# Second attention: which of its small steps run on GpSimd and which on VectorE

## The reference

```
Q, K, V   = xn @ wq, xn @ wk, xn @ wv              16 heads of 8
local     = windowed causal softmax attention, window 32
GQ        = xn @ wgq;  latents = mean of each 4 tokens of xn -> 64 latents
GK, GV    = latents @ wgk, latents @ wgv           8 heads of 8
remote    = causal softmax attention of GQ over the latents, @ r_out_w
x        += (sigmoid(gate_l) * local + sigmoid(gate_r) * remote) @ w_out + MoE(xn)
MoE(xn)   = shared expert * sigmoid(xn @ shared_gate_w)
            + top-8 of 64 experts, weights w / sum(w), at most 64 tokens an expert
```

## Time and profile before

| | us |
|---|---|
| median of 3 runs | 1795.48 (1791.98 to 1797.09) |
| the profiled execution's own time | 1784.54 |
| its span, first to last instruction | 1782.8 |
| second attention, first xT to last pooled batch | 985.8 to 1576.6 |

### The profile page before, as it was taken

One profiled execution on the slowest core, in us unless ns is written; L12 is line 12 of the kernel. 1 busy time (PEld: TensorE's weight loads), 2 busy tenths in 40 slices (PEclk: granted clock), 3 DMA queues, 4 the chain that ended last, 5 costly groups with the idle time before them and its releaser, 6 DMA issues. The chain is left out here.

```text
span 1782.8 us, 43704 instructions
## 1 busy us (share of the span) xinstructions
PE 1623.9 (91%) x13929; PEld 1198.6 (67%) x13931; DVE 1143.2 (64%) x2695; ACT 1007.7 (57%) x2546; POOL 832.5 (47%) x1413
## 2 busy tenths in 40 slices
PE   4799999999999999989996899999999999995883
PEld 4655555555555555547996688888888888884772
DVE  3356555555555555543443699999999999995661
ACT  3355555555555555543442677777777777762341
POOL 5235555555555555553444444444444444412664
PEclk9999999999999999999998799999999999996676
DMA  7412221222222212212221112112111111115444
GB/s 194 128 31 76 55 55 54 54 54 54 54 54 54 54 54 54 54 47 83 65 65 44 31 43 43 40 38 43 41 40 41 43 40 41 43 35 109 96 84 118
DMA packets 207886, 107.45 MB, mean 60 GB/s; under 512 B 102745, under 2 KB 196250, under 8 KB 207770
## 3 DMA queue, kind: packets, MB, share of 16 engines
q1 hardware_dynamic: 197594, 93.16, 20.9%
q0 software_dynamic: 10240, 13.64, 3.5%
HBM read 61.85 MB, written 40.16 MB: 57 GB/s over the span
## 5 line engine op out<-in xcount | busy, mean ns | idle before, releaser
L662 POOL TENSOR_SCALAR_AFFINE_SELECT probs<-probs 128x512 f32<-128x512 f32 x256 | 183.8, 742 | 157.4 <-ACT probs L1446 157.3
L899 DVE TENSOR_REDUCE mneg<-bankS 128x2 f32<-128x256 f32 x256 | 107.5, 420 | 215.1 <-PE bankS L1778 193.7
L1446 ACT ACTIVATE probs<-bankT 128x1024 f32<-128x1024 f32 x128 | 131.1, 1025 | 180.7 <-PE bankT L1798 180.7
L900 DVE TENSOR_REDUCE mneg<-bankS 128x2 f32<-128x512 f32 x256 | 174.6, 682 | 0.0
L1437 ACT ACTIVATE qT<-bankA,bd 128x256 f32<-128x256 f32 x256 | 107.7, 474 | 89.8 <-PE bankA L1760 89.8
L1760 PE MATMUL bankA<-xnT,wd 128*128 128x256 f32 x512 | 149.6, 416 | 0.0
L655 POOL CAST qb<-qT 128x256 bf16<-128x256 f32 x256 | 97.7, 400 | 95.2 <-ACT qT L1437 95.0
L1812 PE MATMUL bankB<-probs,vaug 128*64 128x512 f32 x512 | 140.2, 626 | 1.1 <-ACT yT L1453 1.0
L1795 PE MATMUL bankT<-qT,kT 37*128 37x512 f32 x512 | 136.7, 610 | 3.5 <-DMA qT<-mT 1.8
L1542 ACT ACTIVATE pe<-pr 128x768 f32<-128x768 f32 x128 | 108.2, 845 | 28.2 <-DVE pr L1240 26.0
L1246 DVE STREAM_TRANSPOSE pt<-pe 128x768 f32<-128x768 f32 x128 | 123.8, 967 | 0.4 <-ACT pe L1542 0.2
(11 more groups left out here) (317 smaller groups left out, 4640.8 us busy)
## 6 DMA issues: line engine op xcount, KB each, us to landing
rzb<-reciprocals SPq DMA_DIRECT2D x128, 128.0 KB
yT<-yT SPq DMA_DIRECT2D x64, 128.0 KB
xtab<-tab SPq DMA_DIRECT2D x32, 192.0 KB, 2.0
xs_sorted<-zeros SPq DMA_DIRECT2D x1, 4608.0 KB, 19.2
qT<-xs_sorted SPq DMA_DIRECT2D x36, 128.0 KB, 2.1
ys_sorted<-qT SPq DMA_DIRECT2D x36, 128.0 KB, 1.8
value_rows<-vrow SPq DMA_DIRECT2D x32, 128.0 KB, 1.8
vx<-value_rows SPq DMA_DIRECT2D x256, 16.0 KB, 1.8
```

The source lines that it names most:

```text
L662: pool.affine_select(out=blocks, in_=blocks, compare_op=ALU.is_ge, fill=0.0, base=0, pattern=[[0, 4], [1, P]], channel_multiplier=-1).then ...
L899: dve.tensor_reduce(mneg[:, n.half, 0, :, j], bankS[:, :, 0:128], AX.X, ALU.max, negate=True)
L900: dve.tensor_reduce(mneg[:, n.half, 1, :, j], bankS[:, :, 128:384], AX.X, ALU.max, negate=True).then_inc(S["red_done"], 1)
L1446: act.activation(pT[:, g % 2].rearrange("p e j t -> p e (j t)"), bankT[:, 0:2, :], ACT.Exp, scale=SCALE0).then_inc(S["exp_done"], 1)
```

## The change

Five small steps of the second attention go from DVE to POOL. The pooling of latents is made of two additions of neighbours, with the new tile `xq` between. The two reciprocals are made with a power of -1, from a new constant tile `minus`. The sum of the gated parts moves as it is. Of the weighing, the reduction over the experts stays on DVE (`weight_sum`), and the mask product, `sgc`, the inversion and the product with it move. POOL gets a `step1` of its own, in which the moved functions stand among the old ones: pooling (n), stream (m), gated sum (p), weighing (n), norm (m), weights (n), scaling of rows (b), stream added (b), gather (k = b + 3). The semaphore `x1_copied` goes (its signal is now in `x1_done`) and `top8` comes.

```
@@ gpsimd
             def normalise_rows(b):
+                pool.wait_ge(S["rows_sb"], 2 * b.b + 2)
+                passed(pool)
+                pool.tensor_tensor(recd[:, :, :].rearrange("p s h -> p (s h)"), dens[:, :, :].rearrange("p s h -> p (s h)"),
+                                   minus[:, 0:1].to_broadcast([P, 4 * SL]), ALU.pow).then_inc(S["rd_done"], 1)
                 pool.wait_ge(S["rows_sb"], 2 * b.b + 3)
                 pool.wait_ge(S["rd_done"], b.b + 1)
...
+            def pool_latents(n):
+                pool.wait_ge(S["tT_sb"], n.b + 1)
+                passed(pool)
+                pairs = xT1[:, n.half, :].rearrange("p (m k) -> p m k", k=2)
+                pool.tensor_tensor(xq[:, :], pairs[:, :, 0], pairs[:, :, 1], ALU.add).then_inc(S["xp_done"], 1)
+                pool.wait_ge(S["xp_done"], n.b * 2 + 1)
+                pairs = xq[:, :].rearrange("p (m k) -> p m k", k=2)
+                pool.tensor_tensor(xp[:, n.half, :], pairs[:, :, 0], pairs[:, :, 1], ALU.add).then_inc(S["xp_done"], 1)
+
+            def gated_sum(b):
+                pool.wait_ge(S["comb"], b.b * 2 + 2)
+                passed(pool)
+                pool.tensor_tensor(aT[:, :], at1[:, :], at2[:, :], ALU.add).then_inc(S["aT_done"], 1)
+
+            def weigh(n):
+                u = n.half
+                pool.wait_ge(S["ex_done"], n.b + 1)
+                pool.wait_ge(S["M_done"], n.b + 1)
+                passed(pool)
+                pool.tensor_scalar(sgc[:, u, :], tsg[:, :], 0.5, 0.5, ALU.mult, ALU.add)
+                pool.tensor_tensor(exl[:, :, :], exl[:, :, :], mb[:, u], ALU.mult).then_inc(S["rstep"], 1)
+
+            def weights(n):
+                u = n.half
+                pool.wait_ge(S["rstep"], n.b * 3 + 2)
+                passed(pool)
+                pool.tensor_tensor(wsum[:, 1, :], wsum[:, 0, :], minus[:, 0:1].to_broadcast([P, 2]), ALU.pow).then_inc(S["rstep"], 1)
+                pool.wait_ge(S["rstep"], n.b * 3 + 3)
+                pool.tensor_tensor(tab[:, u, :, C:C + E1], exl[:, :, :], wsum[:, 1, :].unsqueeze(2).to_broadcast([P, 2, E1]),
+                                   ALU.mult).then_inc(S["tab_done"], 1)
+
+            def step1(b, p, n, m, k):
+                if n:
+                    pool_latents(n)
+                if m:
+                    stream1(m)
+                if p:
+                    gated_sum(p)
+                if n:
+                    weigh(n)
+                if m:
+                    norm1(m, True)
+                if n:
+                    weights(n)
+                if b:
                     normalise_rows(b)
                     add_stream(b)
-                    gather(b.next().next().next())
+                if k:
+                    gather(k)
...
             stream1(second)
+            pool_latents(first)
+            weigh(first)
+            norm1(second, False)
+            weights(first)
+            gather(Batch(1, 0))
@@ vector
-            def pool_latents(n):
-                dve.wait_ge(S["tT_sb"], n.b + 1)
-                dve.tensor_reduce(xp[:, n.half, :], xT1[:, n.half, :].rearrange("p (n k) -> p n k", k=CHUNK), AX.X,
-                                  ALU.add).then_inc(S["xp_done"], 1)
...
-            def weigh(n):
...
+            def weight_sum(n):
+                dve.wait_ge(S["rstep"], n.b * 3 + 1)
+                passed(dve)
                 dve.tensor_reduce(wsum[:, 0, :], exl[:, :, :], AX.X, ALU.add).then_inc(S["rstep"], 1)
...
-            def invert1(b):
-                dve.wait_ge(S["rows_sb"], 2 * b.b + 2)
-                dve.reciprocal(recd[:, :, :], dens[:, :, :]).then_inc(S["rd_done"], 1)
...
-                dve.wait_ge(S["comb"], b.b * 2 + 2)
-                dve.tensor_tensor(aT[:, :], at1[:, :], at2[:, :], ALU.add).then_inc(S["aT_done"], 1)
```

More of the change, by code:

```diff
@@ L543, in _ @@
             pool.memset(halfneg[:, :], -0.5)
+            pool.memset(minus[:, :], -1.0)
             pool.memset(owr[:, :], 0.0).then_inc(S["zeroed"], 1)
@@ L829, in _ @@
[L829 to L840, removed]
@@ L841, in _ @@
-            add_stream(Batch(LOOP, 1))
+                if k:
+                    gather(k)
+            first, second = Batch(0, 0), Batch(0, 1)
+            gather(first)
+            gather(second)
+            clear()
+            stream1(first)
+            norm1(first, False)
+            stream1(second)
+            pool_latents(first)
[3 more added lines that the diff above has]
+            gather(Batch(1, 0))
+            step1(first, None, second, Batch(1, 0), Batch(1, 1))
@@ new lines, in _ @@
+            step1(second, first, Batch(1, 0), Batch(1, 1), Batch(2, 0))
+            with pool.Fori(1, LOOP - 1) as i:
+                step1(Batch(i, 0), Batch(i, 0).before(), Batch(i, 1), Batch(i + 1, 0), Batch(i + 1, 1))
+                step1(Batch(i, 1), Batch(i, 0), Batch(i + 1, 0), Batch(i + 1, 1), Batch(i + 2, 0))
+            step1(Batch(LOOP - 1, 0), Batch(LOOP - 2, 1), Batch(LOOP - 1, 1), Batch(LOOP, 0), Batch(LOOP, 1))
+            step1(Batch(LOOP - 1, 1), Batch(LOOP - 1, 0), Batch(LOOP, 0), Batch(LOOP, 1), None)
@@ L843, in _ @@
+            step1(Batch(LOOP, 0), Batch(LOOP - 1, 1), Batch(LOOP, 1), None, None)
+            step1(Batch(LOOP, 1), Batch(LOOP, 0), None, None, None)
+            gated_sum(Batch(LOOP, 1))
             for u in range(2):
@@ L1216, in route @@
                 dve.tensor_tensor(mb[:, u], lg1[:, :, 0:E1], lgr[:, :, :], ALU.not_equal).then_inc(S["M_done"], 1)
-            def weigh(n):
-                u = n.half
-                dve.wait_ge(S["ex_done"], n.b + 1)
-                dve.wait_ge(S["M_done"], n.b + 1)
-                dve.tensor_tensor(exl[:, :, :], exl[:, :, :], mb[:, u], ALU.mult).then_inc(S["rstep"], 1)
-                dve.wait_ge(S["rstep"], n.b * RSTEPS + 2)
-                dve.tensor_reduce(wsum[:, 0, :], exl[:, :, :], AX.X, ALU.add).then_inc(S["rstep"], 1)
-                dve.wait_ge(S["rstep"], n.b * RSTEPS + 3)
-                dve.reciprocal(wsum[:, 1, :], wsum[:, 0, :]).then_inc(S["rstep"], 1)
-                dve.wait_ge(S["rstep"], n.b * RSTEPS + 4)
-                dve.tensor_scalar(sgc[:, u, :], tsg[:, :], 0.5, 0.5, ALU.mult, ALU.add)
-                dve.tensor_tensor(tab[:, u, :, C:C + E1], exl[:, :, :], wsum[:, 1, :].unsqueeze(2).to_broadcast([P, 2, E1]),
-                                  ALU.mult).then_inc(S["tab_done"], 1)
+            def weight_sum(n):
+                dve.wait_ge(S["rstep"], n.b * 3 + 1)
+                passed(dve)
+                dve.tensor_reduce(wsum[:, 0, :], exl[:, :, :], AX.X, ALU.add).then_inc(S["rstep"], 1)
             def shift(b, g):
@@ L1308, in step1 @@
                 if n:
-                    weigh(n)
+                    weight_sum(n)
                 if b:
```

24 lines of the change are left out of this document (11 added, 13 removed).

## The result

The changed kernel takes 2108.01 us (median of 4 runs, 2102.68 to 2111.21), the kernel before, run beside it, 1796.28: a ratio of 1.174, 95% interval 1.170 to 1.177, slower by 17%. The forecast was 2137 with a range of 2000 to 2235. The profiled execution has a span of 2100.6 in place of 1782.8 (+317.8) and a mean granted clock of 0.896 of full speed in place of 0.955.

What follows compares the result with a forecast made beforehand. Loop bound by DVE for two thirds and PE for one, 19.15 us a step. Added: 29 steps x 10.95 = 318, last two 15, tail 5.9 and 0.4, start 3, together 342; 1784.5 to 2126.5, plus 10.9: 2137 us, range 2000 to 2235.

Steps and rivals of the forecast that it cites:

- The power, 8.0 us: POOL's inversion of the denominators over 128x48: 0.41 us fixed plus 0.158 a column, 8.0 us against 0.45 on DVE.
- The walk: One loop step followed through POOL's queue from the fourth probability transpose: 30.1 us a step, 10.95 more than before.
- the 0.2 for the clock: PE idle from +6.1 to +13.4, then remote, queries and scores at up to twice their time; 0.2 us a step added.
- start and end: Start: weigh(0) before norm1(1), pooling of batch 1 behind a gather, some 3 us; tail: rows scaled 5.9 later, slower sum 0.4.
- the last two steps: Loop steps without a gather: 2 x (10.95 - 3.5) = 15 us more.
- the median: Median of the runs shown taken as 10.9 us above the profiled execution, raising 2126.5 to 2137.
- the path through pooling and ACT's copies: Pooling behind the gather until +18.1, ACT's copies to +28.0, last exponential and fourth transpose: +29.9, setting the step.
- that through the gated sum: Gathered rows +18.8, stream +21.0, gated sum +21.9, projection, DVE's last addition +23.1, next fourth transpose about +29.6.
- the two pieces that leave the chain: DVE's pooling reduction, 0.42 us, and final gated sum, 0.40: 25 us if nothing else moved; not subtracted in the forecast.
- The first rival: Power over 48 columns costs 0.5 to 2 us: step 22.6 at the lower bound, 1899 us, up to 1940; 10%.
- The signs: In the loop: POOL busy two thirds, DVE idle 8 us, ACT 10, clock below 1.00, chain of waits mostly POOL.
- a curve that flattens: Power below 8.0 us: cheap, 0.5 to 2 us, 10%; or slope falling with length, 3 to 6.5 us, 1970 to 2085, 9%.

Runs made afterwards that it cites:

- experiment 5: Changed kernel with a probe ahead of the second attention, POOL powers over 1 to 96 columns, twice each, and additions: 2193.06 us, one run.
- Experiment 4: Changed kernel with the gated sum put ahead of the next batch's stream in POOL's queue: 2086.57 us, ratio 1.165 to the kernel before.
- experiment 3: Kernel before with only the denominators' inversion as POOL's power, plus unread products on PE in its wait: 22 products 2079.03 us, 12 products 1967.39 us.
- Experiment 1: Changed kernel with the inversion of the denominators back on DVE as a reciprocal: 1896.78 us, ratio 1.058 to the kernel before.
- experiment 6: Changed kernel, inversion on DVE, pooling before gather, sum before stream: 1794.29 us; sum also on DVE: 1782.90; kernel before with only pooling on POOL, before gather: 1784.41.
- experiment 2: Kernel before with one move alone, the denominators inverted by POOL's power: 2044.35 us, ratio 1.142.
- experiments 6 to 8: After experiment 6: its 1782.90 us kernel with index copies ahead of pooling, 1778.18 us; then changed kernel with POOL and DVE operations timed side by side, 2123.97 us.

## Why the prediction was right, and where it was not

**The power, 8.0 us.** Right: 8010 ns. Two rows of one operation at two sizes gave slope and offset, and experiment 5 shows the same line from 1 to 96 columns. The Trainium skill's 2.6 cycles an element (GPSIMD Engine Reference, section 3.1) fails here by far: 0.159 us at 1.2 GHz are an estimated 190 cycles a column.

**The walk.** From the end of the fourth transpose, forecast and trace: weights done +3.7, +3.3; power +11.8, +11.3; rows scaled +12.75, +12.3; gather +17.0, +16.4; pooling +18.1, +17.2; ACT's string of copies over +28.0, +26.8. Each is a little early: POOL did not wait ahead of the weights' power and only 0.08 behind it (0.35 was allowed for both), the products over 128x128 took 0.40 and not 0.46, pooling 0.77 and not 1.1, and ACT's string 9.5 and not 9.85. The end from there was 0.4 longer than forecast, for the wait of the next paragraph, and the 0.2 for the clock is not seen. Together that is the 1.08 us by which the step was over-estimated (30.1 forecast, 29.02 measured). Over 29 steps it is some 31 us. The rest nearly cancels, which is luck: start and end cost 18.6 and not 9.3 (6.6 of it in stages that the change doesn't touch), the last two steps 13 and not 15, and the median lay 5.3 above the profiled execution where I had added 10.9. So the time was 29 too high.

**Which way round is the longer.** Named wrongly. I gave the path through pooling and ACT's copies +29.9 and that through the gated sum +29.6. In the trace ACT waits 0.41 for DVE ahead of the last exponential, and DVE's last addition, which ends at +22.3 (forecast +23.1), had waited for the projection of the gated sum:

```profile
1421.26 0.42 DVE L1310 TENSOR_TENSOR res<-bankT,res 128x256 f32<-128x256 f32 x1 [0.71 <-PE bankT L2132]
```

```profile
1426.52 0.84 ACT L1568 ACTIVATE pe<-pr 128x768 f32<-128x768 f32 x1 [0.41 <-DVE pr L1275]
```

Experiment 4 takes the sum's path away and gains just about that, 0.45. For the time it makes no difference here; for someone who wants to mend the kernel it is the difference between moving pooling and moving the sum.

**The clock.** I saw the idle stretch and the half clock after it, and then wrote that what runs slowly has slack until +20, and added 0.2. For the power alone that is too small: experiment 3 shows 2.6 us a step (27.3 against 24.7), since DVE waits for the scores in bank S, and my term would have been off by 75 us. For the whole change the slack was there: ACT's string starts when POOL has pooled and then runs without a gap, and PE is back at full clock before the gated sum comes. So the stretch lies under pooling's wait (power alone 27.3 with the clock in it, the whole change 29.0). That is read from the trace; no run keeps PE busy in the changed kernel.

**What the other moves cost.** The earlier trace rows offered 0.8 us a step for the two pieces that leave the chain. Against it stood the place in POOL's queue: pooling behind a gather that holds the queue for 3.5 us. Experiment 1 measures that as +3.3 a step, experiment 6 as the same 3.3 given back by a reordering. The first rival (a step of 22.6 for a cheap power) is borne out in kind by 22.4, but the closeness is partly luck: its walk gives 21.9 for a power that costs nothing and has no term for the clock, and in experiment 1 the clock fell in 19 of 29 steps.

**The signs.** POOL is busy 68% of a step, DVE waits 7.4 us a step and ACT 10, both for POOL, and the step's clock is 0.82, all as forecast. One sign did not come: the page's chain of waits is not mostly POOL (PE 4% of the span, POOL 3%). It goes back only to the last steps of the stage, whose powers it holds, and so tells nothing of the loop; the step from one scaling to the next had to serve in its place.

**Chances.** Between cheap and dear power I kept 19% for a curve that flattens. Two rows at 2 and 8 columns can't rule it out, so that was fair.

## What to carry to other kernels

Before an operation moves to another engine, find that very operation there at two sizes: an addition of 48 columns and a power of 48 columns differ by thirty on GpSimd. Then read the target's queue and not its busy share: an engine with 10 us to spare in 19 is late for everybody if the new work stands behind a gather or ahead of what another engine waits for, and another order of that queue was worth some 100 us here, with the same work in it. Where another engine leaves TensorE idle, count with its products after the gap at half speed: after a wait of 6 us it was so in every step (experiment 2), after one of 2 us in 19 of 29 (experiment 1).

## What the runs showed of the hardware

- An operation of VectorE over 128 columns between SBUF tiles, 0.22 to 0.29 us alone, is held up until GpSimd's operation has ended where that is an addition, a scaling by constants or a copy. It costs 0.4 to 0.5 us more beside an addition of 256 columns and 0.2 beside a scaling or copy (experiments 6 to 8). GpSimd's power, 2.3 us for 12 columns, does not do this, nor its scaling of the normed batch, beside which VectorE's product stayed at 0.28. VectorE's transposes stayed at 0.97 beside GpSimd's addition (29 times in the kernel before). The Trainium skill (SBUF — State Buffer, section "SBUF: two separate sides") has a port pair that the two engines share under an exclusive lock, taken on VectorE's side by operations with two SBUF inputs or in a two-port mode. The traces agree for the two-input operations beside additions, constant scalings and copies, down to the end of `mb` 0.15 us after the addition's. By that rule VectorE's scaling in experiment 8 would be in a two-port mode, which no run here tests, and the power and the scaling of the normed batch, which both read SBUF, should lock VectorE out for their length, which they did not.
- A product of 128 by 128 with 128 by 256 in float32 shows as two passes of 0.22 us each at full clock, 9.77 us for 22 of them (experiment 3).
- In the changed kernel's step the granted clock was 0.50 from 1412.3 to 1417.0, with PE busy without a gap, 0.71 from 1417 to 1418 and 1.00 from there on. With PE kept busy until the rows came it was 1.00 over 1100 to 1750 (experiment 3, 12 products).
- The same wait does not always cost the clock: in experiment 1, waits of PE of 1.9 to 2.1 us were followed by full clock in 10 of 29 steps and by a fall to 0.50 in the other 19.
